# First layer's head of a four-stage hybrid kernel: one transfer for the projection, two folds in a row, the first batch in halves

## The chip, the cores and the metric

The kernel runs on one core of a Trainium2 chip, in float32 with some products in 16 bits. The metric is the device time of one execution in microseconds (us). In this text PE is TensorE, DVE is VectorE, ACT is ScalarE, POOL is GpSimd and SP is SyncE. Each runs its own list of instructions in order and waits on semaphores.

## What is computed

`x` is 2 batches of 512 rows with 256 channels. Four stages follow each other: attention, a feed-forward part, a state-space convolution, and the feed-forward part again, each with its own layer norm of what it reads. The change is in the first:

```python
x_norm = (x - mu) / jnp.sqrt(var + EPS) * gamma + beta
q = x_norm @ qkv[:, :KEY]
k = x_norm @ qkv[:, KEY:2 * KEY]
v = x_norm @ qkv[:, 2 * KEY:]
scores = jnp.einsum('bsk,btk->bst', q, k) * scale      # causal
attn = jax.nn.softmax(scores, axis=-1)
out = (attn @ v) @ o_proj + residual
```

The feed-forward part rounds its weights to an 8-bit grid first (`w.astype(jnp.float8_e4m3fn)`) and then computes `(silu(x @ gate * s) * (x @ up * s)) @ down * s`.

## The kernel before

The order of each engine's work is written out by hand; nothing reorders it. The 1,024 rows of `x` are eight tiles of 128 rows, numbered 0 to 7, four to a batch; the 256 channels are two chunks of 128.

**Head.** Instead of `q` and `k`, the kernel multiplies the weights once: `wqk` from `Wq` and `Wk`, `wvo` from `Wv` and `o_proj` (a "fold", L1047). Then the scores are `xn wqk xn^T` and the values `xn wvo`. For a fold PE turns the three thirds of `qkv` (`turn_w`, L1039) and ACT copies each from PSUM (`turned`, L492). Of `x`, DVE takes the statistics of two tiles at a time (`first_stats`, L707), POOL the inverse deviation (`inverse_std`, L285). Tiles 0 to 3 are normalised on DVE (`normalise`, L701), tiles 4 to 7 on ACT (L529). PE turns them (`turn_z`, L1054), and ACT (chunk 0) and DVE (chunk 1) apply gamma and beta on the way out of PSUM, giving `xn_cols` (`xn_chunk`, L497 and L712). `make_g` (L1062) gives `g = xn wqk` with 512 columns at a time, copied by `g_part` on ACT and `g_chunk` on DVE; `make_v` (L1071) gives the values, copied half by ACT (`v_part`), half by DVE (`v_half`, L723).

**Attention.** Per tile k: `scores(k)` on PE, `row_max(k)` on DVE (L853), the exponential on ACT (L562), `turn_probs(k)` on PE, `copy_probs(k)` on ACT, `attend(k)` on PE, `attention_out(k)` on DVE (L858). PE's order is `scores(k)`, `attend(k-2)`, `turn_probs(k-1)` (L1173); ACT's is `exp_scores(k)`, then `copy_probs(k-1)` (L592); DVE's is `row_max(k)`, then `attention_out(k-2)` (L897).

**Weights beside it.** While attention runs, the feed-forward weights are rounded. DVE makes a grid for each of the three weights, as two steps over 1,536 columns (`grid_begin`, `grid_end`, L773 to L781). For gate and up, POOL then adds and subtracts it in three pieces of 512 columns each (`round_weight`, L404); for down, DVE does that itself, with two operands in SBUF (`lift_down`, `lower_down`, L785 to L796). POOL also makes the scales of the residual (`x_plus_scales`, L393).

**Loads.** SP issues x, the thirds of `qkv`, the four parameter rows, `o_proj`, the scales and the weights on one queue (L238 to L251); ACT issues three small ones (L513 to L518), POOL two (L383). PE runs 14 transposes of the identity at the start and 8 more between the turning of q and of k (L1037, L1080).

## Time and profile before

| | us |
|---|---|
| median of 3 runs | 127.24 |
| lowest and highest | 127.01, 127.3 |
| the profiled execution | 127.35 |
| its span | 125.6 |
| PE busy in the span | 116.5 (93%) |
| DVE busy | 94.4 (75%) |
| POOL busy | 86.8 (69%) |
| ACT busy | 77.6 (62%) |

The head and the attention take the first 52 us of the span; the rest is the feed-forward parts and the convolution. The chain of waits follows the work that ended last back from the end, each step to what released it. A timeline row is a group of instructions in a row on an engine, with its start, its length and, in brackets, how long the engine stood idle before it and what ended that. The trace shows two records for each float32 product of PE (one for each transpose), the lists of the order one.

### The profile page before, as it was taken

The page shows a single profiled execution, that of the slowest core. Times are in us where ns is not written, and L with a number is a line of the kernel's source. Part 1 is how long each engine was busy: PE and PEld are TensorE (multiplying, and loading weights), DVE is VectorE, ACT ScalarE, POOL GpSimd, SP SyncE. Part 2 cuts the span into 40 slices and gives each one's busy share as a digit, 9 for nine tenths or more (in the row PEclk, how much of TensorE's full clock was granted, in tenths as well). Part 3 has the DMA queues.
Part 4 walks back from the last instruction along what each step waited for, and adds up shares of the span by engine and source line. Part 5 has one row for each costly group of instructions (what it writes and reads, how often), then busy time and mean ns, then how long its engine had stood idle before and what let it go on. Part 6 is the DMA issues. An engine that isn't in the chain of part 4 may idle for free.

```text
span 125.6 us, 2089 instructions
## 1 busy us (share of the span) xinstructions
PE 116.5 (93%) x666; PEld 77.3 (62%) x666; DVE 94.4 (75%) x226; ACT 77.6 (62%) x147; POOL 86.8 (69%) x168
## 2 busy tenths in 40 slices
PE   5997999999999999999999999989999869999970
PEld 5885468658668758745769545567446457556640
DVE  0398999919865866949797899947899946784592
ACT  2145079695875468858865278865578764579800
POOL 2246469999999888888433578889978870038831
PEclk9999999999999999999999999999999999999999
DMA  3998940000000000000000000000000000000404
GB/s 90 297 277 322 354 135 8 0 0 0 0 0 0 5 5 0 0 0 0 0 0 5 0 0 0 0 3 5 0 0 0 3 0 0 5 0 24 143 0 167
DMA packets 5682, 5.80 MB, mean 46 GB/s; under 512 B 1140, under 2 KB 5160, under 8 KB 5672
## 3 DMA queue, kind: packets, MB, share of 16 engines
q1 hardware_dynamic: 4648, 5.52, 13.3%
q10 hardware_dynamic: 960, 0.15, 0.7%
q8 instruction: 5, 0.08, 0.3%
q14 instruction: 5, 0.04, 0.1%
q0 software_dynamic: 64, 0.02, 0.1%
HBM read 4.63 MB, written 1.05 MB: 45 GB/s over the span
## 4 chain that ended last, share of the span: by engine, by line
PE 66%; DVE 11%; POOL 10%; ACT 4%; issue 3%; DMA 3%; SPq 0%; POOLq 0%; DVEq 0%; ACTq 0%
PE psum L1195 22%; PE psum L1211 10%; PE psum L1134 7%; PE psum L1109 7%; PE psum L1074 6%; POOL rstd L296 4%; DMA qkv_sb<-in_qkv 3%; PE psum L1067 3%; DVE stats L696 3%; PE psum L1156 2%; PE psum L1122 2%; POOL f_tail L451 2%; ACT h_rows L559 2%; ACT normed L529 2%; PE psum L1050 2%
## 5 line engine op out<-in xcount | busy, mean ns | idle before, releaser
L607 ACT ACTIVATE gated<-psum,scales 128x512 f32<-128x512 f32 x24 | 16.3, 681 | 13.1 <-PE psum L1195 13.1
L451 POOL TENSOR_TENSOR f_tail<-fused,f_head 128x512 f16<-128x512 f32 x12 | 14.1, 1173 | 12.8 <-ACT f_head L613 12.5
L1211 PE MATMUL psum<-down,f_head 128*128 128x256 bf16 x96 | 22.1, 273 | 0.5 <-POOL f_tail L451 0.5
L1211 PE MATMUL psum<-down,f_tail 128*128 128x256 bf16 x96 | 22.0, 272 | 0.0
L958 DVE SCALAR_TENSOR_TENSOR fused<-psum,up_scales_fit,gated 128x512 f32<-128x512 f32 (+1 forms) x25 | 17.8, 716 | 4.6 <-PE psum L1195 3.3
L613 ACT ACTIVATE f_head<-fused 128x512 f16<-128x512 f32 (+1 forms) x25 | 15.1, 606 | 3.4 <-DVE fused L958 3.2
L966 DVE TENSOR_TENSOR f_tail<-fused,f_head 128x512 f16<-128x512 f32 (+1 forms) x13 | 9.7, 749 | 9.2 <-ACT f_head L613 9.1
L1195 PE MATMUL psum<-h_head,up 128*128 128x512 f16 x48 | 14.3, 379 | 0.0
L1195 PE MATMUL psum<-h_tail,up 128*128 128x512 f16 x48 | 14.3, 379 | 0.0
L1195 PE MATMUL psum<-h_tail,gate 128*128 128x512 f16 x48 | 14.3, 379 | 0.0
L1195 PE MATMUL psum<-h_head,gate 128*128 128x512 f16 x48 | 14.3, 379 | 0.0
L296 POOL TENSOR_TENSOR rstd<-var_eps,neg_half 128x2 f32<-128x2 f32 (+1 forms) x15 | 12.3, 822 | 2.2
L1211 PEld LDWEIGHTS psum<-down,f_head 128*128 128x128 f16 x96 | 9.4, 98 | 4.2 <-POOL f_tail L451 1.8
L1134 PE MATMUL psum<-v_rows,probs_cols 128*128 128x256 f32 x40 | 10.3, 389 | 0.2 <-ACT probs_cols L575 0.2
L1211 PEld LDWEIGHTS psum<-down,f_tail 128*128 128x128 f16 x96 | 9.4, 98 | 1.6
L1109 PE MATMUL psum<-xn_cols,g_cols 128*128 128x128 f32 (+3 forms) x32 | 10.0, 436 | 0.0
L291 POOL TENSOR_SCALAR var_eps<-mean_var 128x2 f32<-128x2 f32 (+1 forms) x15 | 3.8, 255 | 8.8 <-DVE mean_var L699 7.7
L1134 PEld LDWEIGHTS psum<-v_rows,probs_cols 128*128 128x128 f32 x40 | 7.0, 190 | 2.3 <-ACT probs_cols L575 0.8
L1195 PEld LDWEIGHTS psum<-h_tail,gate 128*128 128x128 f16 x48 | 4.7, 98 | 5.7 <-DVE h_tail L850 0.2
L1195 PEld LDWEIGHTS psum<-h_tail,up 128*128 128x128 f16 x48 | 4.7, 98 | 5.7
L1195 PEld LDWEIGHTS psum<-h_head,up 128*128 128x128 f16 x48 | 4.7, 98 | 5.6
L1067 PE MATMUL psum<-xn_cols,wqk 128*128 128x512 f32 x16 | 7.4, 604 | 0.7 <-DVE xn_cols L715 0.7
(167 smaller groups left out, 257.2 us busy)
## 6 DMA issues: line engine op xcount, KB each, us to landing
x_in<-in_x SPq DMA_DIRECT2D x4, 256.0 KB, 4.2
qkv_sb<-in_qkv SPq DMA_DIRECT2D x3, 256.0 KB, 4.0
gate_raw<-in_gate_w SPq DMA_DIRECT2D x1, 768.0 KB, 6.8
up_raw<-in_up_w SPq DMA_DIRECT2D x1, 768.0 KB, 8.6
down_raw<-in_down_w SPq DMA_DIRECT2D x1, 768.0 KB, 10.3
out<-x_in SPq DMA_DIRECT2D x3, 256.0 KB, 2.1
wo_sb<-in_o_proj SPq DMA_DIRECT2D x1, 256.0 KB, 5.3
down_scale_all<-in_down_scale SPq DMA_DIRECT2D x1, 128.0 KB, 10.1
```

The costliest lines, as they stand in the source:

```text
L296: power = pool.tensor_tensor(rstd[:, n, k:k + count], var_eps[:, n, k:k + count], neg_half[:, 0:count], ALU.pow)
L451: pool.tensor_tensor(f_tail[:, m, :], fused[:, m % FUSED, :], f_head[:, m, :], ALU.subtract).then_inc(f_tail_by_pool, 1)
L607: act.activation(gated[:, m % 2, :], psum[:, BANK_GATE[m % 2], :], ACT.Silu, scale=gate_scales[:, m:m + 1]).then_inc(gated_ready, 1)
L613: act.activation(f_head[:, m, cols], fused[:, m % FUSED, cols], ACT.Copy).then_inc(f_head_ready, 1)
L958: dve.scalar_tensor_tensor(out=fused[:, m % FUSED, cols], in0=psum[:, BANK_UP[m % 2], cols], scalar=up_scales_fit[:, m:m + 1], in1=gated[: ...
L966: dve.tensor_tensor(f_tail[:, m, cols], fused[:, m % FUSED, cols], f_head[:, m, cols], ALU.subtract).then_inc(f_tail_by_dve, 1)
L1067: last = pe.matmul(column(BANK_G[b][j], 0, S), wqk[:, c, j * P:j * P + P], xn_cols[:, b, c, :], start=(c == 0), stop=(c == C - 1))
L1074: last = pe.matmul(column(BANK_V[b][t // 2], H * (t % 2), H), xn_cols[:, b, c, t * P:t * P + P], wvo[:, c, :], start=(c == 0), stop=(c == ...
L1109: pe.matmul(column(BANK_S[k % 2], 0, W), g_cols[:, b, j, i * P:i * P + P], xn_cols[:, b, j, 0:W], start=(j == 0), stop=(j == C - 1))
L1134: last = pe.matmul(column(BANK_O[k % 2], 0, H), probs_cols[:, k % 2, t * P:t * P + P], v_rows[:, b, t, :], start=(t == 0), stop=(t == i))
L1195: last = pe.matmul(column(banks[m % 2], 0, S), w[:, c, m * P:m * P + P], part[:, c, :], start=(part is h_head and c == 0), stop=(part is h ...
L1211: last = pe.matmul(down_columns(n, t), part[:, m, t * P:t * P + P], down16[:, m, :], start=(m == 0 and (t % 2 == 0 or n == 2 * B - 1) and ...
```

## The change

- SP loads the whole `qkv` in one transfer behind the first x, then x1, `o_proj`, x2, x3. Three parameter rows (gamma, beta, d) go to ACT's queue, ahead of its own loads; the fourth, `log_dt`, which nothing read, is gone. The two `c` loads go from POOL to the end of SP's queue.
- PE makes 17 warm-up transposes and none in between. It turns all three thirds in a row and makes both folds in a row. The copy of the turned k goes from ACT to DVE (`copy_k`).
- The first batch goes by halves of its tokens: `turn_z_half`, `xn_half` on ACT and DVE, `make_g_half` with 256 columns. The first half of `g` is copied by ACT alone, the second by DVE alone. `scores(0)` and `scores(1)` come ahead of the second half of `g`, of the values and of the second batch's `z`. `make_g_half(1)` writes the bank of the first values, so it waits for `v_by_act`.
- DVE copies the parameters, the turned k and the first half of `xn` ahead of `first_stats(2)`; `row_max(0)` and `row_max(1)` come ahead of the grids of up and down.
- POOL makes `x_plus_scales` ahead of `round_weight(0)`. ACT makes both first exponentials ahead of the last copy of `g` and the second square.

```diff
-WARM_UP = 14
-WARM_BETWEEN = 8
+WARM_UP = 17
...
-        BANK_G = [[6, 7], [0, 1]]
+        BANK_G = [[5, 2], [0, 1]]
...
             load_x(0)
-            load_chunks(qkv_sb[:, :, 0:KEY], qkv[:, 0:KEY], q_loaded)
+            load_chunks(qkv_sb[:], qkv, qkv_loaded)
             load_x(1)
-            load_chunks(qkv_sb[:, :, KEY:2 * KEY], qkv[:, KEY:2 * KEY], k_loaded)
-            load_rows(param_rows, (gamma, beta, log_dt, d_param), params_loaded)
-            load_chunks(qkv_sb[:, :, 2 * KEY:], qkv[:, 2 * KEY:], v_loaded)
+            load_chunks(wo_sb[:], o_proj, wo_loaded)
             load_x(2)
             load_x(3)
-            load_chunks(wo_sb[:], o_proj, wo_loaded)
             load_rows(scale_rows, (gate_scale, up_scale), scales_loaded)
             load_chunks(gate_raw[:], gate_w, w_loaded[0])
             load_chunks(up_raw[:], up_w, w_loaded[1])
             load_chunks(down_raw[:], down_w, w_loaded[2])
+            for n, array in ((2, c_re), (3, c_im)):
+                load_chunks(s4d_in[:, n, :].rearrange("p (c n) -> p c n", c=C), array, c_loaded)
             sp.dma_start(down_scale_all[:], down_scale.partition_broadcast(P)).then_inc(down_scale_loaded, 16)
...
-                load_s4d(2, c_re, c_loaded)
-                load_s4d(3, c_im, c_loaded)
...
             inverse_std(0, T, T, twice=True, negative_mean=True)
+            x_plus_scales()
             round_weight(0, gate16, gate_up_ready)
-            x_plus_scales()
             angle_squares()
...
+            def load_row(n, vector):
+                act.dma_start(param_rows[C * n:C * n + C, :],
+                              vector.rearrange("(m p) -> m p", p=P)).then_inc(params_loaded, 16)
...
+            load_row(0, gamma)
+            load_row(1, beta)
+            load_row(2, d_param)
...
             turned(0)
-            turned(1)
+            turned(2)
+            xn_half(0)
+            act.wait_ge(wqk_made, 1)
+            act.activation(wqk[:].rearrange("p c n -> p (c n)"), psum[:, BANK_WQK, :], ACT.Copy).then_inc(wqk_ready, 1)
+            act.wait_ge(wvo_made, 1)
+            act.activation(wvo[:].rearrange("p c n -> p (c n)"), psum[:, BANK_WVO, :], ACT.Copy).then_inc(wvo_ready, 1)
+            g_first_half()
...
+            xn_half(1)
...
-            act.wait_ge(wvo_made, 1)
-            act.activation(wvo[:].rearrange("p c n -> p (c n)"), psum[:, BANK_WVO, :], ACT.Copy).then_inc(wvo_ready, 1)
-            g_part(0)
-            xn_chunk(1)
+            v_part(0)
...
             act.activation(s4d[:, 12, 0:HN], s4d[:, 9, 0:HN], ACT.Sin, scale=0.5).then_inc(trig_out, 1)
-            v_part(0)
+            xn_second()
...
             exp_scores(0)
-            g_part(1)
+            exp_scores(1)
+            g_part()
             square_weights(1)
-            exp_scores(1)
...
+            def copy_k():
+                dve.wait_ge(w_turned_pe, 2)
+                dve.tensor_copy(w_turned[:, 1, :, :].rearrange("p c n -> p (c n)"),
+                                psum[:, BANK_WT[1], :]).then_inc(k_turned, 1)
+
+            def copy_params():
+                dve.wait_ge(params_turned, 1)
+                dve.tensor_copy(params[:], psum[:, BANK_PARAMS, 0:3 * C]).then_inc(params_ready, 1)
                 dve.wait_ge(params_ready, 1)
...
+            def xn_half(half):
+                dve.wait_ge(z_turned, half + 1)
+                dve.tensor_scalar(xn_cols[:, 0, 1, HALVES[half]], psum[:, BANK_Z[0][1], HALVES[half]], gammas[:, 1:2],
+                                  betas[:, 1:2], ALU.mult, ALU.add).then_inc(xn_by_dve, 1)
...
+            def g_second_half():
+                dve.wait_ge(g_made, 2)
+                dve.tensor_scalar(g_cols[:, 0, :, HALVES[1]], psum[:, BANK_G[0][1], :].rearrange("p (j s) -> p j s", j=C),
+                                  float(KEY) ** -0.5, None, ALU.mult).then_inc(g_by_dve, 1)
...
             first_stats(0)
             normalise((0, 1))
+            copy_params()
+            copy_k()
+            xn_half(0)
             first_stats(2)
+            first_stats(T)
+            normalise((2, 3))
+            first_stats(T + 2)
             exp_reduce()
-            normalise((2, 3))
-            dve.wait_ge(params_turned, 1)
-            dve.tensor_copy(params[:], psum[:, BANK_PARAMS, 0:4 * C]).then_inc(params_ready, 1)
+            xn_half(1)
             exp_finish()
-            xn_chunk(0)
-            first_stats(T)
-            first_stats(T + 2)
             exp_times_dt()
             reduce_angle()
             grid_begin(0)
             grid_end(0)
-            g_chunk(0)
+            row_max(0)
+            row_max(1)
+            g_second_half()
+            xn_second()
+            v_half(0)
             grid_begin(1)
-            xn_chunk(1)
             grid_end(1)
             grid_begin(2)
-            v_half(0)
-            row_max(0)
             grid_end(2)
-            row_max(1)
             lift_down(0)
-            g_chunk(1)
+            g_chunk()
             lift_down(1)
             lower_down(0)
             v_half(1)
...
+            def turn_w(w):
+                pe.wait_ge(qkv_loaded, 16)
...
+            def turn_z_half(half):
+
+                for t in (2 * half, 2 * half + 1):
+                    pe.wait_ge(z_ready, t + 1)
+                    for c in range(C):
+                        last = pe.transpose(column(BANK_Z[0][c], t * P, P),
+                                            normed[:, t, c * P:c * P + P], ident[:])
+                last.then_inc(z_turned, 1)
...
+            def make_g_half(half):
+
+                columns_there(half + 1)
                 for j in range(C):
                     for c in range(C):
-                        last = pe.matmul(column(BANK_G[b][j], 0, S), wqk[:, c, j * P:j * P + P], xn_cols[:, b, c, :],
+                        last = pe.matmul(column(BANK_G[0][half], j * (S // 2), S // 2), wqk[:, c, j * P:j * P + P],
+                                         xn_cols[:, 0, c, HALVES[half]], start=(c == 0), stop=(c == C - 1))
+                last.then_inc(g_made, 1)
...
-            turn_w(0, q_loaded)
-            warm_up(WARM_BETWEEN)
-            turn_w(1, k_loaded)
-
-            pe.wait_ge(params_loaded, 64)
-            pe.transpose(column(BANK_PARAMS, 0, 4 * C), param_rows[:], ident[0:4 * C, 0:4 * C]).then_inc(params_turned, 1)
-            turn_z(0, (0, 1))
-            pe.wait_ge(w_turned_ready, 2)
+            turn_w(0)
+            turn_w(1)
+            turn_w(2)
+
+            pe.wait_ge(params_loaded, 48)
+            pe.transpose(column(BANK_PARAMS, 0, 3 * C), param_rows[:], ident[0:3 * C, 0:3 * C]).then_inc(params_turned, 1)
+            turn_z_half(0)
+            pe.wait_ge(q_v_turned, 1)
+            pe.wait_ge(k_turned, 1)
             fold(BANK_WQK, 0, lambda kc: w_turned[:, 1, kc, :]).then_inc(wqk_made, 1)
-            turn_z(0, (2, 3))
-            turn_w(2, v_loaded)
-            pe.wait_ge(wqk_ready, 1)
-            pe.wait_ge(params_ready, 1)
-            make_g(0)
-            pe.wait_ge(w_turned_ready, 3)
+            pe.wait_ge(q_v_turned, 2)
             pe.wait_ge(wo_loaded, 16)
             fold(BANK_WVO, 2, lambda kc: wo_sb[:, kc, :]).then_inc(wvo_made, 1)
+            pe.wait_ge(wqk_ready, 1)
+            make_g_half(0)
+            turn_z_half(1)
+            pe.wait_ge(wvo_ready, 1)
+            make_v(0, (0, 1))
...
+                if k == 2:
                     pe.wait_ge(g_by_dve, 1)
...
                 if k == 0:
-                    pe.wait_ge(v_by_act, 1)
+                    pe.wait_ge(g_by_dve, 1)
                     pe.wait_ge(v_by_dve, 1)
...
-            turn_z(1)
-            pe.wait_ge(wvo_ready, 1)
-            make_v(0)
             scores(0)
-
+            scores(1)
+            pe.wait_ge(v_by_act, 1)
+            make_g_half(1)
+            turn_z()
+            make_v(0, (2, 3))
+
+            columns_there(3)
             pe.wait_ge(scales_loaded, 32)
-            pe.wait_ge(xn_by_act, 2)
             pe.transpose(column(BANK_SCALES, 0, 2 * M), scale_rows[:], ident[0:2 * M, 0:2 * M]).then_inc(scales_turned, 1)
-            make_g(1)
-            scores(1)
+            make_g()
             turn_probs(0)
             pe.wait_ge(scales_ready, 1)
             make_v(1)
```

DVE between its first `normalise` and the end of the second, before: L704 is `normalise`, L696 and L699 are statistics, L734 to L747 an exponential, L874 the copy of the parameters.

```order
L704 TENSOR_SCALAR normed<-x_in,mean_var,rstd 128x256 x2
L696 BN_STATS stats<-x_in 128x6 x2
L699 BN_AGGR mean_var<-stats 128x2 x2
L734 TENSOR_SCALAR s4d<-e_in 128x18
L735 TENSOR_SCALAR s4d<-s4d 128x18
L736 SCALAR_TENSOR_TENSOR s4d<-s4d,e_in 128x18
L737 SCALAR_TENSOR_TENSOR s4d<-s4d 128x18
L738 TENSOR_SCALAR s4d<-s4d 128x18
L739 TENSOR_SCALAR two_k<-s4d 128x18
L704 TENSOR_SCALAR normed<-x_in,mean_var,rstd 128x256 x2
L874 COPY params<-psum 128x8
```

And now, where L713 is `normalise`, L728 the parameters, L723 `copy_k`, L733 `xn_half`, L705 and L708 statistics.

```order
L713 TENSOR_SCALAR normed<-x_in,mean_var,rstd 128x256 x2
L728 COPY params<-psum 128x6
L723 COPY w_turned<-psum 128x512
L733 TENSOR_SCALAR xn_cols<-psum,params 128x256
L705 BN_STATS stats<-x_in 128x6 x2
L708 BN_AGGR mean_var<-stats 128x2 x2
L705 BN_STATS stats<-x_in 128x6 x2
L708 BN_AGGR mean_var<-stats 128x2 x2
L713 TENSOR_SCALAR normed<-x_in,mean_var,rstd 128x256 x2
```

The copies of the parameters and of k, which wait for PE, now stand ahead of the statistics of all tiles but the first two; the exponential stands behind them.

DVE from the first `g` copy to the second, before: L776 and L781 are the grids, L715 `xn_chunk`, L725 `v_half`, L855 `row_max`, L789 `lift_down`.

```order
L720 TENSOR_SCALAR g_cols<-psum 128x512
L776 TENSOR_SCALAR grid<-up_raw 128x1536
L715 TENSOR_SCALAR xn_cols<-psum,params 128x512
L781 TENSOR_SCALAR grid<-grid 128x1536
L776 TENSOR_SCALAR grid<-down_raw 128x1536
L725 COPY v_rows<-psum 128x512
L855 TENSOR_REDUCE neg_max<-psum 128x1
L781 TENSOR_SCALAR grid<-grid 128x1536
L855 TENSOR_REDUCE neg_max<-psum 128x1
L789 TENSOR_TENSOR down_raw<-down_raw,grid 128x768
L720 TENSOR_SCALAR g_cols<-psum 128x512
```

And now, from `row_max(0)` on: L883 is `row_max`, L743 and L748 copies of `g`, L738 `xn_second`, L753 `v_half`, L804 and L809 the grids, L817 `lift_down`.

```order
L883 TENSOR_REDUCE neg_max<-psum 128x1 x2
L743 TENSOR_SCALAR g_cols<-psum 128x2x256
L738 TENSOR_SCALAR xn_cols<-psum,params 128x512
L753 COPY v_rows<-psum 128x512
L804 TENSOR_SCALAR grid<-up_raw 128x1536
L809 TENSOR_SCALAR grid<-grid 128x1536
L804 TENSOR_SCALAR grid<-down_raw 128x1536
L809 TENSOR_SCALAR grid<-grid 128x1536
L817 TENSOR_TENSOR down_raw<-down_raw,grid 128x768
L748 TENSOR_SCALAR g_cols<-psum 128x512
L817 TENSOR_TENSOR down_raw<-down_raw,grid 128x768
```

The four grid steps of up and down, which had copies and row maxima between them, now stand in a row behind `v_half(0)`.

PE from the first `g` to the second batch's, before: L1067 is `make_g`, L1050 a fold, L1058 `turn_z`, L1074 `make_v`, L1109 and L1111 scores, L1167 the turned scales.

```order
L1067 MATMUL psum<-xn_cols,wqk 128x512 x4
L1050 MATMUL psum<-wo_sb,w_turned 128x256 x4
L1058 MATMUL psum<-ident,normed 128x128 x8
L1074 MATMUL psum<-wvo,xn_cols 128x256 x8
L1109 MATMUL psum<-xn_cols,g_cols 128x128 x2
L1111 MATMUL psum<-mask,ident 128x128
L1167 MATMUL psum<-ident,scale_rows 128x12
L1067 MATMUL psum<-xn_cols,wqk 128x512 x4
```

And now: L1109 is `make_g_half`, L1096 and L1087 turn `z`, L1123 is `make_v`, L1161 and L1163 scores, L1221 the scales, L1116 `make_g`.

```order
L1109 MATMUL psum<-xn_cols,wqk 128x256 x4
L1096 MATMUL psum<-ident,normed 128x128 x4
L1123 MATMUL psum<-wvo,xn_cols 128x256 x4
L1161 MATMUL psum<-xn_cols,g_cols 128x128 x2
L1163 MATMUL psum<-mask,ident 128x128
L1161 MATMUL psum<-xn_cols,g_cols 128x256 x2
L1163 MATMUL psum<-mask,ident 128x128
L1109 MATMUL psum<-xn_cols,wqk 128x256 x4
L1087 MATMUL psum<-ident,normed 128x128 x8
L1123 MATMUL psum<-wvo,xn_cols 128x256 x4
L1221 MATMUL psum<-ident,scale_rows 128x12
L1116 MATMUL psum<-xn_cols,wqk 128x512 x4
```

Two tiles of scores now stand ahead of the second halves of `g` and `v` and of the second batch's `z`.

## Rows read from the trace of the kernel before

**Rows 1.** Chain of waits (start us, us, what), 7 to 39 us.

```profile
7.37 0.44 PE psum L1043 x4
...
13.48 0.26 DVE mean_var L699 x2
...
16.49 2.09 ACT normed L529 x4
...
23.48 3.63 PE psum L1067 x8
...
28.15 3.46 PE psum L1074 x16
31.60 1.29 PE psum L1109 x4
...
37.41 1.56 PE psum L1134 x6
```

**Rows 2.** Window 37.40 to 52.45: its length, PE busy (instructions), clock, DMA.

```profile
37.40:52.45 15.05, 15.04 (x96) 1.00 0.01 2
```

**Rows 3.** Landing of `qkv`; issue of k on SP's queue; the page's GB/s.

```profile
DMA to landing us min/median/max: 3.7/4.0/4.3
...
2.23 0.47 SPq L229 DMA_DIRECT2D qkv_sb<-in_qkv  x1
...
GB/s 90 297 277 322 354 135 8 0 0 0 0 0 0 5 5 0 0 0 0 0 0 5 0 0 0 0 3 5 0 0 0 3 0 0 5 0 24 143 0 167
```

**Rows 4.** Timeline of PE, the first 6 us.

```profile
1.52 3.25 PE L1035 MATMUL psum<-ident 128*128 128x128 f32 x14 [1.52 <-POOL ident L277]
4.98 1.12 PE L1043 MATMUL psum<-ident,qkv_sb 128*128 128x128 f32 x4 [0.21 <-DMA qkv_sb<-in_qkv]
```

**Rows 5.** Timeline of DVE, two groups of its head.

```profile
6.68 0.74 DVE L696 BATCH_NORM_STATS2 stats<-x_in 128x6 f32<-128x256 f32 x2
...
15.44 0.95 DVE L776 TENSOR_SCALAR grid<-gate_raw 128x1536 uint32<-128x1536 uint32 x1
```

**Rows 6.** Timelines of DVE and POOL, weight steps, 17 to 42 us.

```profile
17.91 1.65 DVE L776 TENSOR_SCALAR grid<-up_raw 128x1536 uint32<-128x1536 uint32 x1
...
20.65 1.99 POOL L408 TENSOR_TENSOR x<-gate_raw,grid 128x512 f32<-128x512 f32 x1
...
21.43 2.03 DVE L776 TENSOR_SCALAR grid<-down_raw 128x1536 uint32<-128x1536 uint32 x1
...
32.86 3.73 POOL L408 TENSOR_TENSOR scaled_down<-up_raw,grid 128x512 f32<-128x512 f32 x3
...
40.14 1.08 DVE L795 TENSOR_TENSOR down_raw<-down_raw,grid 128x768 f32<-128x768 f32 x1
...
40.49 0.78 POOL L291 TENSOR_SCALAR var_eps<-mean_var 128x2 f32<-128x2 f32 x1
41.35 0.19 POOL L293 TENSOR_SCALAR mean_rstd<-mean_var 128x2 f32<-128x2 f32 x1
```

**Rows 7.** Timeline of POOL, first long and last step of `x_plus_scales`.

```profile
28.13 1.66 POOL L396 TENSOR_TENSOR rstd<-var_eps,neg_half 128x8 f32<-128x8 f32 x1
...
31.13 0.79 POOL L399 TENSOR_SCALAR neg_x_plus<-mean_rstd 128x8 f32<-128x8 f32 x1
```

**Rows 8.** Timeline of DVE, 23 to 36 us.

```profile
23.38 0.68 DVE L725 COPY v_rows<-psum 128x512 f32<-128x512 f32 x1
...
28.07 0.42 DVE L855 TENSOR_REDUCE neg_max<-psum 128x1 f32<-128x256 f32 x1 [2.67 <-PE psum L1111]
...
32.98 0.56 DVE L855 TENSOR_REDUCE neg_max<-psum 128x1 f32<-128x384 f32 x1 [0.53 <-PE psum L1111]
...
34.63 0.18 DVE L699 BATCH_NORM_AGGREGATE mean_var<-stats 128x2 f32<-128x6 f32 x1
...
35.47 0.69 DVE L855 TENSOR_REDUCE neg_max<-psum 128x1 f32<-128x512 f32 x1 [0.66 <-PE psum L1111]
```

77 lines of the change are left out of this document (40 added, 37 removed).

## The prediction, made before the changed kernel was run

> **What bounds the kernel now.** Start with the chain of waits. From 19 us on it is TensorE (PE) alone: the two big products of the second batch, 3.63 and 3.46 us, and the scores of tile 2 at 31.60 follow each other without a gap [rows 1]. Ahead of that it is a relay: the first third of `qkv`, 3.7 us after its issue [rows 3], transposes, a fold, then at 13.48 VectorE's (DVE's) statistics, POOL, and ScalarE's (ACT's) four `normed` rows until 18.58 [rows 1]. The next view is PE by windows: from 37.40 to 52.45, where the feed-forward part begins, PE is busy 15.04 of 15.05 us [rows 2]. So whatever the head loses or gains by the time `attend(2)` starts (37.41 [rows 1]) is handed on whole. The last view is DVE's timeline: it waits 2.67 us for the scores of tile 1 [rows 8], so today DVE's weight work (`grid`, `lift`, `lower`) is paid out of idle time. That is the number to keep an eye on, because the change moves this work.
>
> **The transfer and the start.** The three thirds of `qkv` landed 3.7, 4.0 and 4.3 us after issue, the first being 3.7, and the second was issued at 2.23, so it was there at 6.2 to 6.5 [rows 3]. By then the queue had moved x0, q, x1 and k, 1,024 KB, the same bytes as x0 and the whole `qkv`. I take 6.35 for the new landing. Worked out another way, `qkv` is 786,000 bytes behind x0 (there at 3.7): at the 354 GB/s of the page's fifth slice that is 2.2 us, 5.9; at the 277 of the third 2.8 us, 6.5, and 0.3 more if the first bytes come late, 6.8 [rows 3]. PE's 17 warm-up transposes at 3.25/14 = 0.23 us are over by 5.5, so PE waits about 0.9 us. Twelve transposes at 0.44 per four [rows 1] are 1.3 us, with 0.2 for the first two, as the clock was still at its lower level until about 6.7: four transposes at 4.98 took 1.12 us [rows 4]. They end at 7.9, the parameters' transpose and `z` half 0 at 8.5. Loads that move to ACT's queue: three issues put its table load 1.5 us later, to about 5 us, and its first copy is wanted at 7.2, so that costs nothing; the two `c` loads leave POOL and land behind `down_raw`, long before `taps_begin`: nothing.
>
> **PE to its first stop.** The fold now needs `copy_k` from DVE, and DVE stands at `copy_params` from 6.7 (it began `first_stats(2)` at 6.68 before [rows 5]) until the parameters are turned at 8.2. 0.15 and 0.6 us (a 512-column PSUM copy is 0.68 [rows 8]) later, at 9.1, the fold starts. From there in a row: the fold's 8 matmuls of 256 columns, 1.73 by the 3.46 us for 16 [rows 1] and 0.15 to start, 1.9; second fold 1.73, `make_g_half(0)` 1.73, `z` half 1 0.44, `make_v` on two tiles 1.73, scores 0 and 1 1.4: 18.0. Then PE waits for `v_by_act`. DVE, 9.05: `xn_half` 0.4, two `first_stats` 1.9, `normalise` 0.9, the last statistics 1.0, 13.2. From there to ACT's first `normed` took 13.74 to 16.49 = 2.75 us and the four took 2.09 [rows 1]; with `v_part` 0.6 this is 18.7. PE: wait 0.7, `g` half 1 1.73, `turn_z` 0.87, `make_v` 1.73: second half of `v` at 23.2. Then 0.16, 3.5 and 3.6 us: `scores(2)` starts at about 30.3, against 31.60 [rows 1]. **By PE alone the change gains 1.3 us.**
>
> **DVE, where I think it is lost.** `grid_begin(0)` started at 15.44 [rows 5]. Now DVE has stood 1.5 us at `copy_params` and made an extra 0.6 us copy, so it starts at 18.1 and ends the pair at 20.0; `round_weight(0)` on POOL starts at 20.1 (`x_plus_scales`, now ahead of it, took from about 28 to 31.9 [rows 7] and would run 16.0 to 20.1). Two row maxima, `g_second_half` and `xn_second` follow, then DVE waits for `v` until 23.2 and is free at 23.9. Only now come `grid` 1 and 2, the two lifts, `g_chunk`, the lower and `v_half(1)`, and behind them `row_max(2)`.
>
> How long is that? Alone, a `grid` piece is 0.95 us [rows 5] and a POOL piece 3.73/3 = 1.24 [rows 6]. Side by side they were 1.65 and 2.03 on DVE and 1.99 on POOL [rows 6]. The ends tell why: the POOL piece of 20.65 ended at 22.64, the DVE piece that had been asked for at 21.43 ended 0.82 later, at 23.46. They do not slow each other, they take turns, and a DVE piece that finds POOL at the start of a piece costs that piece without its start-up, 1.24 less 0.1, and its own 0.82: 1.95 us. Before, PSUM copies lay between the DVE pieces and hid POOL's turns; now four stand in a row. The two-input steps take turns too: `lower_down(1)` at 40.14 took 1.08 and POOL's small step at 40.49 took 0.78 until DVE was done [rows 6], when the like step at 41.35 took 0.19.
>
> The sum from 23.9: POOL's first three pieces are just over (20.1 + 3.7), so `grid_begin(1)` 0.95; three more at 1.95 each, against POOL's other three, 5.85; `lift_down(0)` 0.9 beside POOL's small angle steps (as long as a `grid` piece alone, less the overlap with the next), `g_chunk` 0.6, `lift_down(1)` 0.9; by 32.3 POOL has begun on `up`, so `lower_down(0)` takes a turn behind it, 1.95; `v_half(1)` 0.6. `row_max(2)` starts at 35.65 against 32.98 [rows 8], although its scores are there at 31.7. Next: `row_max(3)` stands behind `attention_out(0)`, 1.8 us (32.98 to the end of the statistics at 34.81 [rows 8]), so 37.45. From its start to `attend(2)` took 35.47 to 37.41, 1.94 us [rows 1, 8], through ACT's exponential and copy. `attend(2)` starts at 39.4 against 37.41: **+1.9 to 2.0 us**. I take 1.9, as the halves of `xn` may be a shade shorter than I allowed. PE's waits behind it were 0.01 us [rows 2], so nothing is given back. The profiled execution (127.35) would become 129.25, the median of the runs, 0.11 lower, 129.1.
>
> The Trainium skill (SBUF — State Buffer, Who interferes with whom) says the same of the pair: VectorE in a two-port mode, or with two SBUF inputs against a GpSimd step that reads SBUF, and GpSimd hold a shared port pair one at a time, and the second "fully blocks". By that rule, the trace agrees: 2.03 us for a 0.95 us step. The rule speaks against putting DVE's `grid` pieces back to back beside POOL's. It also names the two-input steps: without a turn for `lower_down(0)` the sum would be 1 us lower, 128.1.
>
> **Rivals.** (1) *Faster: the turns do not bite.* If POOL and DVE run past each other (POOL late or early by its six pieces), DVE's block from 23.9 is 4 x 0.95 + 2.9 + 1.2 = 7.9 us, over at 31.8, as the scores of tile 2 land. Then PE's gain of 1.3 stands: 125.9. It decides at the point where the block is under 8 us. For it: the row of [rows 5] at 0.95. Against it: POOL's six pieces are six times 1.24 = 7.5 us from 20.1, so they must overlap it. (2) *Half the price:* the two-input steps escape POOL's second round because it starts later than 33: 1.1 us less, 128.0. (3) *The clock rises later.* PE was busy almost without a break from 1.52 until it rose [rows 4]; now it stands idle from 5.5 to 6.4. If it stays at the lower level for the transposes and the first fold (0.23 to 0.28 against 0.11 a transpose), 1.2 us are added: 130.3. (4) *Nothing:* DVE's block of about 9.7 us eats exactly PE's gain, 127.2. That one transfer lands later than two thirds did is in the range (0.25 us of the sum for 0.45 of landing, since part is under `v_by_act`).
>
> **Chances.** Forecast, with its ends at 128.3 and 129.9: 50%. Rival 3: 14%. Rival 2: 12%. Rival 1: 16%. Rival 4 or close to it: 8%. A measurement here can tell about 0.2% (0.25 us). So slower by more than that 76%, the same 8%, faster 16%. The range leaves out rival 1 and the worst of rival 3: 127.4 to 130.6.
>
> **What would show it.** Right: in the profile of the changed kernel `grid` pieces of L804 and L809 take about 2 us in three of the last four, `row_max(2)` starts near 35.6, PE has a wait of some 3 us ahead of `attend(1)` whose releaser is ACT's `probs_cols`, behind DVE's `neg_max`, and `scores(2)` starts near 30.3 all the same. The `qkv` landing is at 5.9 to 6.8 and the fold starts near 9.1. Wrong: `row_max(2)` waiting for its scores instead of being late for them (rival 1), or twelve transposes that take over 2 us (rival 3).

## The result, and the profile of the changed kernel

The change makes the kernel slower, and by far more than forecast.

| kernel | median us | lowest to highest | ratio to before |
|---|---|---|---|
| before | 127.16 | 127.01 to 127.30 | |
| changed | 133.18 | 131.31 to 134.18 | 1.037 (1.031 to 1.043) |

The ratio is taken over undisturbed executions alone, so it is lower than the quotient of the medians. The profiled execution took 132.64 us with a span of 130.8, against 127.35 and 125.6: 5.3 us more.

The first thing to look at is the page's line of PE's granted clock, in 40 slices of the span, for before and then for the changed kernel. A 9 stands for 90% of full speed or more.

```profile
PEclk9999999999999999999999999999999999999999
PEclk9999999999965799999999999999999999999997
```

The timeline of PE in the changed kernel (start us, us, engine, line, operation, tiles, count, and in brackets the idle time ahead with its releaser) shows where that is:

```profile
29.73 1.45 PE L1161 MATMUL psum<-xn_cols,g_cols 128*128 128x384 f32 x4
...
33.51 0.22 PE L1163 MATMUL psum<-mask,ident 128*128 128x128 bf16 x1
37.99 2.07 PE L1186 MATMUL psum<-v_rows,probs_cols 128*128 128x256 f32 x4 [4.27 <-ACT probs_cols L584]
39.86 0.85 PE L1174 MATMUL psum<-ident,probs 128*128 128x128 f32 x3
...
41.46 2.81 PE L1186 MATMUL psum<-v_rows,probs_cols 128*128 128x256 f32 x6
...
57.58 0.59 PE L1248 MATMUL psum<-h_head,gate 128*128 128x512 f16 x2
```

The same places in before:

```profile
31.44 1.45 PE L1109 MATMUL psum<-xn_cols,g_cols 128*128 128x384 f32 x4
...
35.27 1.08 PE L1134 MATMUL psum<-v_rows,probs_cols 128*128 128x256 f32 x4
...
37.41 1.56 PE L1134 MATMUL psum<-v_rows,probs_cols 128*128 128x256 f32 x6 [0.23 <-ACT probs_cols L575]
...
52.28 0.59 PE L1195 MATMUL psum<-h_head,gate 128*128 128x512 f16 x2
```

And PE by windows in the changed kernel (start and end, length, PE busy with its instructions, granted clock, DMA share, GB/s):

```profile
29.73:33.72 3.99, 3.99 (x15) 1.00 0.00 0
33.72:37.99 4.27, 0.01 (x1) 0.91 0.00 0
37.99:44.11 6.12, 6.12 (x19) 0.50 0.00 0
44.11:57.75 13.64, 13.64 (x91) 1.00 0.01 2
```

`scores(2)` does start earlier, at 29.73 against 31.44. But then PE stands for 4.27 us ahead of attend(1), and when it may go on, the clock is granted at 0.50, the lower of its two levels (1.2 GHz instead of 2.4), for 6.12 us. The same matmuls (attend(1), three transposes, `scores(4)`, attend(2)) took 3.30 us at the full clock in before, 35.27 to 38.80 less a wait of 0.23. So the sum up to the feed-forward part, which starts at 57.58 against 52.28, is: -1.71 for the earlier scores, +4.27 for the wait, +2.82 for the clock, -0.23 for the wait that before had there. That is 5.15 of 5.30 us. (The other 0.16 is in the row of windows ahead of the wait: 3.99 us from `scores(2)` on, where before had 3.83 from 31.44 to 35.27.)

DVE's timeline shows what PE waited for:

```profile
7.80 0.17 DVE L728 COPY params<-psum 128x6 f32<-128x6 f32 x1 [1.09 <-PE psum L1133]
8.00 0.69 DVE L723 COPY w_turned<-psum 128x512 f32<-128x512 f32 x1
...
17.94 0.94 DVE L804 TENSOR_SCALAR grid<-gate_raw 128x1536 uint32<-128x1536 uint32 x1
...
22.58 0.69 DVE L753 COPY v_rows<-psum 128x512 f32<-128x512 f32 x1 [0.86 <-PE psum L1123]
23.19 1.32 DVE L804 TENSOR_SCALAR grid<-up_raw 128x1536 uint32<-128x1536 uint32 x1
24.54 1.91 DVE L809 TENSOR_SCALAR grid<-grid 128x1536 f32<-128x1536 f32 x1
26.37 2.02 DVE L804 TENSOR_SCALAR grid<-down_raw 128x1536 uint32<-128x1536 uint32 x1
28.43 1.92 DVE L809 TENSOR_SCALAR grid<-grid 128x1536 f32<-128x1536 f32 x1
30.38 1.02 DVE L817 TENSOR_TENSOR down_raw<-down_raw,grid 128x768 f32<-128x768 f32 x1
...
31.93 2.04 DVE L817 TENSOR_TENSOR down_raw<-down_raw,grid 128x768 f32<-128x768 f32 x1
33.99 1.90 DVE L823 TENSOR_TENSOR down_raw<-down_raw,grid 128x768 f32<-128x768 f32 x1
...
36.42 0.54 DVE L883 TENSOR_REDUCE neg_max<-psum 128x1 f32<-128x384 f32 x1
...
38.14 0.66 DVE L883 TENSOR_REDUCE neg_max<-psum 128x1 f32<-128x512 f32 x1
```

Five of the seven weight steps last about 1.95 us, where [rows 5] had 0.95 for one alone, and `row_max(2)` comes at 36.42 against 32.98 [rows 8]. POOL's timeline beside it has its `gate` pieces from 19.96 to 29.5 and `up` from 31.88, 0.05 us ahead of DVE's second lift:

```profile
19.96 3.73 POOL L400 TENSOR_TENSOR x<-gate_raw,grid 128x512 f32<-128x512 f32 x3 [1.95 <-DVE grid L809]
23.77 5.76 POOL L403 TENSOR_TENSOR gate<-x,grid 128x512 f16<-128x512 f32 x3
...
31.88 5.13 POOL L400 TENSOR_TENSOR scaled_down<-up_raw,grid 128x512 f32<-128x512 f32 x3
```

### The profile page after: what moved, and what is told of

It reads as the page before. It is cut to its first block, busy times and chain, and to the rows that moved or that the text cites. A ratio compares the mean times of both kernels' runs of the same rounds, so it can differ in the third digit from the quotient of the medians.

```text
span 130.8 us, 2095 instructions
## 1 busy us (share of the span) xinstructions
PE 118.0 (90%) x669; PEld 80.1 (61%) x669; DVE 98.1 (75%) x228; ACT 77.7 (59%) x147; POOL 84.8 (65%) x166
## 3 DMA queue, kind: packets, MB, share of 16 engines
HBM read 4.63 MB, written 1.05 MB: 43 GB/s over the span
## 4 chain that ended last, share of the span: by engine, by line
PE 58%; DVE 19%; POOL 8%; ACT 5%; issue 5%; DMA 3%; SPq 0%; POOLq 0%; DVEq 0%
PE psum L1248 21%; PE psum L1264 10%; PE psum L1186 8%; PE psum L1161 4%; DMA qkv_sb<-in_qkv 3%; POOL rstd L290 3%; DVE grid L809 3%; PE psum L1109 3%; PE psum L1079 3%; DVE grid L804 2%; PE psum L1208 2%; DVE down_raw L817 2%; PE psum L1174 2%; POOL f_tail L443 2%; ACT h_rows L568 2%
## 5 line engine op out<-in xcount | busy, mean ns | idle before, releaser
L1186 PE MATMUL psum<-v_rows,probs_cols 128*128 128x256 f32 x40 | 12.6, 454 | 4.3 <-ACT probs_cols L584 4.3
L290 POOL TENSOR_TENSOR rstd<-var_eps,neg_half 128x2 f32<-128x2 f32 (+1 forms) x15 | 12.8, 856 | 2.2
L1186 PEld LDWEIGHTS psum<-v_rows,probs_cols 128*128 128x128 f32 x40 | 8.3, 226 | 6.8 <-ACT probs_cols L584 4.8
L1161 PE MATMUL psum<-xn_cols,g_cols 128*128 128x128 f32 (+3 forms) x32 | 10.4, 456 | 0.0
L285 POOL TENSOR_SCALAR var_eps<-mean_var 128x2 f32<-128x2 f32 (+1 forms) x15 | 3.2, 216 | 10.5 <-DVE mean_var L708 9.5
L576 ACT ACTIVATE probs<-psum,neg_max 128x128 f32<-128x128 f32 (+3 forms) x8 | 4.2, 526 | 9.7 <-DVE neg_max L883 9.7
```

The costliest lines, as they stand in the source:

```text
L290: power = pool.tensor_tensor(rstd[:, n, k:k + count], var_eps[:, n, k:k + count], neg_half[:, 0:count], ALU.pow)
L576: act.activation(probs[:, k % 2, 0:W], psum[:, BANK_S[k % 2], 0:W], ACT.Exp, bias=neg_max[:, k:k + 1], accum_out=row_sum[:, k:k + 1]).then ...
L1161: pe.matmul(column(BANK_S[k % 2], 0, W), g_cols[:, b, j, i * P:i * P + P], xn_cols[:, b, j, 0:W], start=(j == 0), stop=(j == C - 1))
L1186: last = pe.matmul(column(BANK_O[k % 2], 0, H), probs_cols[:, k % 2, t * P:t * P + P], v_rows[:, b, t, :], start=(t == 0), stop=(t == i))
```

## Experiments on the clock

Theory: the wait costs its own length and then the clock. Rival: the wait alone, with the rest of the loss somewhere else. One kernel leaves every engine but PE as it is in the changed kernel; two make a wait in the kernel before.

**a1_fill**, the changed kernel with work for PE in the wait:

```diff
                 scores(k)
+                if k == 3:
+                    pe.wait_ge(g_by_dve, 2)
+                    for _ in range(34):
+                        pe.transpose(column(BANK_O[1], 0, P), ident[:], ident[:])
                 attend(k - 2)
```

> The changed kernel with 34 transposes of the identity on PE between the scores of tile 3 and attend(1), into the bank that attend(1) will overwrite, so that PE's 4.27 us wait is filled and nothing else moves. Theory (the wait makes PE's clock fall to its lower level for 6.8 us, and that is some 3 us of the loss): attend(1) starts at 38.0 as in the changed kernel, PE's products behind it take the short times, the feed-forward part starts near 55.1 instead of 57.75, and the time is 129.8. Rival (the lateness of DVE alone costs all of it, the clock nothing): 133 as the changed kernel.

Measured: 130.44 us median (128.71 to 131.51), ratio 1.018 (1.012 to 1.023). PE's timeline:

```profile
33.60 3.88 PE L1231 MATMUL psum<-ident 128*128 128x128 f32 x34
38.07 1.13 PE L1186 MATMUL psum<-v_rows,probs_cols 128*128 128x256 f32 x4 [0.59 <-ACT probs_cols L584]
```

attend(1) starts at 38.07, as late as in the changed kernel, but takes 1.13 us instead of 2.07, and the clock of the profiled execution is 1.0 throughout. The feed-forward part starts 2.6 us earlier (55.00) without one useful instruction more. Between the two profiled executions the time falls by as much, from 132.64 to 130.07 us. The clock's share of the loss is 2.6 us, and the theory holds.

**b1_long** and **b2_short**, the kernel before with spare steps on DVE, 17 and 11 of them:

```diff
             v_half(1)
+            for n in range(17):
+                dve.bn_stats(spare[:, n, :], x_in[:, n % K, :])
             for k in range(2, K):
```

> The kernel before with 17 spare statistics steps (5.6 us) on DVE ahead of row_max(2), so that PE waits over 4 us ahead of attend(1), as in the changed kernel; nothing of the change is in it. Clock theory: DVE's lateness costs 4.4 us and the fallen clock about 3 more, 134.5. Rival (no clock): 131.6.

> The same with 11 spare steps (3.6 us): PE waits about 2.3 us ahead of attend(1). Clock theory, if the shorter wait leaves the clock up: 127.2 + 2.4 = 129.6; if the clock falls here too, 132 or more. Rival without a clock: 129.6 as well, so this run only says from which length of the wait the price is paid.

Measured: 132.78 us (132.76 to 133.87), ratio 1.047 (1.043 to 1.050), with 17; 130.00 us (129.30 to 131.03), ratio 1.023 (1.018 to 1.029), with 11. `attend(1)` behind the wait, b1_long's and then b2_short's:

```profile
39.41 1.89 PE L1137 MATMUL psum<-v_rows,probs_cols 128*128 128x256 f32 x4 [4.08 <-ACT probs_cols L576]
```

```profile
37.37 1.13 PE L1137 MATMUL psum<-v_rows,probs_cols 128*128 128x256 f32 x4 [2.12 <-ACT probs_cols L576]
```

A wait of 4.08 us on PE brings the lower clock in a kernel that has nothing of the change in it; here the price was 1.4 us: 132.78 less b2_short's 129.37 (both profiled executions), less the 1.96 us by which the wait is longer. I had expected about 3 us and 134.5, so half of the price did not come: the granted clock was low for 3.18 us here and for 6.12 us in the changed kernel. The low stretch is not of one length, and why is open. After 2.12 us the profiled execution kept its clock. But 2 us are no safe side: of b2_short's other three executions two had a mean clock of 0.987 and 0.980 and took 131.03 and 130.62 us, the third 1.0 and 129.30. (These have no trace, so where in them the clock was low is not shown.)

## Experiments on DVE's block

**a2_order**, the changed kernel with lifts and lowers behind the first attention tiles:

```diff
-            lift_down(0)
             g_chunk()
-            lift_down(1)
-            lower_down(0)
             v_half(1)
...
                 if k == 4:
-                    lower_down(1)
+                    lift_down(0)
+                    lift_down(1)
                     magnitude()
+                if k == 5:
+                    lower_down(0)
+                if k == 6:
+                    lower_down(1)
```

> The changed kernel with DVE's two lifts and the first lower of the down weight moved from ahead of row_max(2) to behind attention_out(2), (3) and (4), where DVE waits anyway. Theory (the changed kernel's loss is DVE's block ahead of row_max(2), in turns with POOL, and the clock that follows from PE's wait): row_max(2) starts at 31.6 with its scores just there, PE waits under 1 us, the clock stays, the feed-forward part starts at 50.6 to 51.0 and the time is 125.4 to 125.8, under the kernel before. Rival (the halves and the single transfer cost by themselves): 127.2 or more.

Measured: 127.07 us (126.55 to 127.46), ratio 0.999 (0.996 to 1.002). Between the profiled executions (132.64 and 126.81) 5.8 us are won back by moving DVE's steps on the `down` weight. In its trace `row_max(2)` stands at 31.33, when its scores are there, and the feed-forward part at 51.75 against 52.28 of before. The four `grid` steps still take turns (1.32 to 2.03 us) but end by 30.2: not the turns by themselves, but the turns with three more steps behind them made `row_max(2)` late. DVE's row, and then three smaller waits of PE:

```profile
31.33 0.54 DVE L883 TENSOR_REDUCE neg_max<-psum 128x1 f32<-128x384 f32 x1
```

```profile
35.57 1.56 PE L1188 MATMUL psum<-v_rows,probs_cols 128*128 128x256 f32 x6 [0.23 <-ACT probs_cols L584]
...
45.25 1.13 PE L1188 MATMUL psum<-v_rows,probs_cols 128*128 128x256 f32 x4 [0.35 <-ACT probs_cols L584]
...
47.79 0.66 PE L1176 MATMUL psum<-ident,probs 128*128 128x128 f32 x4 [0.65 <-ACT probs L576]
```

The first was there before; the other two, 1.0 us, are the lowers, now ahead of the row maxima of tiles 6 and 7. With them the feed-forward part starts 0.75 to 1.15 us later than the expected 50.6 to 51.0, and the expected 125.4 to 125.8 did not come.

**a3_pool_later**: are the turns with POOL the reason that the block is long, or the seven steps as such?

```diff
-            round_weight(0, gate16, gate_up_ready)
             angle_squares()
-            round_weight(1, up16, gate_up_ready)
+            pool.wait_ge(v_by_dve, 2)
+            round_weight(0, gate16, gate_up_ready)
             inverse_std(1, 0, 2, negative_mean=True)
+            round_weight(1, up16, gate_up_ready)
```

> The changed kernel with POOL's rounding of `gate` and `up` begun only when DVE has done `v_half(1)`, so that none of POOL's 128x512 pieces lies beside DVE's block; DVE's order and PE's are untouched. Theory (the turns with POOL made the block long, the wait of 4.27 us it led to took the clock): the four `grid` pieces from 23 us and the three `down` pieces take 0.95 us each, `row_max(2)` waits for its scores at about 31.1 instead of being late at 36.4, PE waits under 1 us ahead of attend(1), the granted clock stays at 1.0 and the time is 125.3 to 126.0. If the block is long for another reason (its place behind `v_half(0)`, its own seven pieces), `row_max(2)` stays behind 34 and the time above 130. POOL's later rounding can cost up to 1 us near 46 us, where `h_rows` needs its small steps.

Measured: 135.59 us (134.29 to 136.20), ratio 1.063 (1.057 to 1.069). The time missed and the mechanism hit. DVE's block and `row_max(2)`:

```profile
22.74 0.95 DVE L805 TENSOR_SCALAR grid<-up_raw 128x1536 uint32<-128x1536 uint32 x1
23.73 0.96 DVE L810 TENSOR_SCALAR grid<-grid 128x1536 f32<-128x1536 f32 x1
...
30.84 0.56 DVE L884 TENSOR_REDUCE neg_max<-psum 128x1 f32<-128x384 f32 x1 [0.23 <-PE psum L1164]
```

With POOL silent every one of the seven steps takes 0.95 us, and the row maximum waits for its scores, as in before. PE ran ahead and met a new wait at the far end:

```profile
55.08 1.12 PE L1209 MATMUL psum<-ident,h_rows 128*128 128x128 f32 x4 [6.94 <-ACT h_rows L569]
```

POOL's later `up` rounding ends at 48.0, and behind it in POOL's queue stand the taps, the weight bound and then the inverse deviations of tiles 2 and 3 that `h_rows` needs, at 52.2. I had put up to 1 us on that place; it was 6.94 us, and the clock fell again behind it (the four transposes took 1.12 us instead of 0.60).

**c1_row**, the kernel before with one part of the change alone, the `grid` steps in a row:

```diff
-            grid_begin(1)
             xn_chunk(1)
-            grid_end(1)
-            grid_begin(2)
             v_half(0)
             row_max(0)
+            grid_begin(1)
+            grid_end(1)
+            grid_begin(2)
             grid_end(2)
             row_max(1)
```

> The kernel before with one part of the change alone: DVE's pieces of `grid` 1 and 2 stand in a row behind `v_half(0)` and `row_max(0)`, ahead of `row_max(1)`. Theory: they start at 24.4; POOL's first six pieces run until 28, so two of the four take 1.3 and 1.95 us and the others 0.95; `row_max(1)` starts at 29.8 (28.07 before), `row_max(2)` 1.7 us late at 34.7, PE waits under 2.1 us and keeps its clock: 128.7 to 129.2. Rival (the order costs nothing, as DVE idles 2.67 us there anyway): 127.2.

Measured: 127.15 us (127.02 to 127.80), ratio 0.999 (0.996 to 1.002). My theory missed by 1.6 to 2 us. DVE and POOL:

```profile
23.37 0.95 DVE L776 TENSOR_SCALAR grid<-up_raw 128x1536 uint32<-128x1536 uint32 x1
24.36 1.91 DVE L781 TENSOR_SCALAR grid<-grid 128x1536 f32<-128x1536 f32 x1
26.19 0.95 DVE L776 TENSOR_SCALAR grid<-down_raw 128x1536 uint32<-128x1536 uint32 x1
```

```profile
20.98 4.47 POOL L411 TENSOR_TENSOR gate<-x,grid 128x512 f16<-128x512 f32 x3
25.54 0.79 POOL L395 TENSOR_SCALAR var_eps<-mean_var 128x8 f32<-128x8 f32 x1
```

One step of four took a turn: with no DVE step between them POOL's pieces ended at 25.45, not 28, and what POOL did next was small. DVE stood there idle anyway. So a row of steps is not the fault by itself. With a3_pool_later it says that the fault is the row at the time of POOL's pieces. In the changed kernel these began at 19.96 instead of 17.47, since `grid_begin(0)` began at 17.94 instead of 15.44 [rows 5].

**a4_x_plus_behind** undoes one part of the change, on POOL:

```diff
-            x_plus_scales()
             round_weight(0, gate16, gate_up_ready)
+            x_plus_scales()
```

> The changed kernel with one part undone: POOL's `x_plus_scales` stands behind its rounding of `gate` again, as before the change. In the changed kernel POOL's six `gate` pieces begin at 19.96 us either way (they wait for `grid`), but its `up` pieces would now begin some 2.5 us later, behind 34 us. Theory: the four `grid` pieces keep their turns, the last two two-input steps (2.04 and 1.90 us in the changed kernel) fall to about 1.0 each, `row_max(2)` moves from 36.4 to 34.5, PE's wait from 4.27 to 2.3 us, and because the wait is shorter the granted clock does not fall: 127.6 to 128.6. Rival (the clock falls after any wait of that kind): 131 and more. Rival (`x_plus` comes too late for attention_out(0) and holds it): wait as long as before, 133.

Measured: 131.00 us (129.12 to 131.44), ratio 1.023 (1.016 to 1.030). DVE did what was expected to 0.1 us, ACT and PE did not. The rows are DVE's, ACT's and PE's:

```profile
32.02 0.95 DVE L817 TENSOR_TENSOR down_raw<-down_raw,grid 128x768 f32<-128x768 f32 x1
33.00 0.96 DVE L823 TENSOR_TENSOR down_raw<-down_raw,grid 128x768 f32<-128x768 f32 x1
...
34.48 0.55 DVE L883 TENSOR_REDUCE neg_max<-psum 128x1 f32<-128x384 f32 x1
```

```profile
34.51 2.08 ACT L561 ACTIVATE x_plus<-x_in,neg_x_plus,one_rstd 128x256 f32<-128x256 f32 x4 [5.32 <-POOL neg_x_plus L391]
```

```profile
37.47 1.95 PE L1186 MATMUL psum<-v_rows,probs_cols 128*128 128x256 f32 x4 [3.58 <-ACT probs_cols L584]
```

The two-input steps lose their turns and `row_max(2)` comes at 34.48. But ACT's four `x_plus` rows now stand ahead of its exponential and start when POOL lets them, so that PE still waits 3.58 us, and the clock falls (1.95 us for 1.08). In the execution of 129.12 us, which has no trace, the mean clock was 1.0. So POOL's new order costs two turns and spares PE this wait for ACT; undoing it gains 1.8 us between the profiled executions (132.64 and 130.85), not the whole 5.3.

## Attempts at a version that beats both

Four kernels build on the changed head. **w1_spread** puts single DVE steps into DVE's waits. **w2_block_free** computes the `grid` of `gate` at 13 us and that of `up` behind the `down` steps, so that POOL rounds ahead of the block and behind it. **w3_taps_behind** adds POOL's inverse deviations ahead of its taps. **w4_warm** adds two warm-up transposes. w2_block_free and the two built on it also have `first_stats(2)` ahead of `copy_params`, as w1_spread has. The core of w2_block_free:

```diff
             exp_reduce()
+            grid_begin(0)
+            grid_end(0)
             xn_half(1)
...
             v_half(0)
-            grid_begin(1)
-            grid_end(1)
             grid_begin(2)
             grid_end(2)
             lift_down(0)
             g_chunk()
             lift_down(1)
             lower_down(0)
+            grid_begin(1)
+            grid_end(1)
             v_half(1)
```

And what w3_taps_behind does on POOL:

```diff
-            taps_begin()
...
             inverse_std(1, 2, 2, negative_mean=True)
+            taps_begin()
```

> The changed kernel with DVE's weight work spread: `first_stats(2)` ahead of `copy_params` (into the wait of 1.09 us), `grid_begin(1)` ahead of `v_half(0)` (into the wait of 0.86 us), `g_chunk` between the `grid` pieces, the lifts and lowers of `down` one by one among the attention tiles (k = 4, 4, 5, 7). Theory: `row_max(2)` waits for its scores (31.1), PE's waits up to 52 us add up to under 1 us, clock 1.0: 125.4 to 126.2. Rival: POOL's turns on the spread pieces hold the row maxima of tiles 5 to 7 back as they did with three pieces (0.2 to 0.7 us each): 126.6 to 127.3.

> The changed kernel with DVE's order changed so that POOL's twelve pieces and DVE's block stand one after the other: `first_stats(2)` ahead of `copy_params`, `grid` of `gate` at about 12.6 us (into DVE's wait for `z`), so that POOL rounds `gate` from 16.4 to 24; behind `v_half(0)` the `down` weight's grid, lifts and lower first and `grid` of `up` last, so that POOL's `up` pieces begin after the block. Theory: the seven pieces of the block take 0.95 us but for the first (a turn at 23 us), `row_max(2)` waits for its scores (31.1), PE has no wait over 1 us, clock 1.0, the feed-forward part begins at 50.5 to 51.5 and the time is 125.3 to 126.3. Rival (another chain takes the gain, as in the run with POOL's rounding later): a wait on `h_rows` near 47 us of over 1 us, 126.5 to 127.5.

> As the kernel with the free block, and on POOL the small steps of the taps (about 3 us) moved behind the inverse deviations of tiles 2 and 3, which ACT's second pair of `h_rows` waits for. Theory: what is left of the wait on `h_rows` near 47 us goes; 125.2 to 125.8, at or below the kernel with the free block. Rival: the taps were hidden there: the same time as that kernel within 0.3 us.

> As the kernel with the taps behind, and 19 warm-up transposes on PE instead of 17 (2 x 0.23 us), which fills the gap of 0.3 to 0.6 us until `qkv` lands. Theory: executions in which PE stands idle there get their full clock later, and these make the spread of the changed kernels (up to 1 us); with the gap filled the spread falls to that of the kernel before (0.3 us) at the same lowest time. Rival: the spread has another cause and stays.

The table has two more kernels, which are told of below it.

| kernel | median us | lowest to highest | ratio to before |
|---|---|---|---|
| w1_spread | 127.40 | 127.19 to 128.11 | 1.002 (1.000 to 1.004) |
| w2_block_free | 127.28 | 126.07 to 128.35 | 1.001 (0.998 to 1.004) |
| w3_taps_behind | 127.29 | 126.20 to 130.02 | 0.999 (0.996 to 1.003) |
| w4_warm | 127.07 | 125.77 to 128.52 | 0.999 (0.996 to 1.002) |
| w5_trig_first | 126.78 | 126.21 to 127.83 | 0.998 (0.996 to 1.000) |
| w6_thirds | 128.43 | 128.15 to 130.24 | 1.017 (1.011 to 1.023) |

The first four miss their expectation, though in their traces DVE's block holds PE up for a quarter of a microsecond at most ahead of `attend(1)` and `attend(2)`; the best executions of the last three of them, 125.77 to 126.20, are near it.

w1_spread's time is its rival's (127.40 for 126.6 to 127.3), but not by the rival's way. PE's waits that the rival named are small (0.26 and 0.60 us), and the feed-forward part starts at 51.57, 0.7 us earlier than in before. That gain is lost 10 us later: `lower_down(1)`, now at 48.35, holds POOL's rounding of `down` back (49.45 for 48.63 in before), some of POOL's small steps behind it take longer too, and POOL ends the taps of the convolution so late (61.43 for 60.15) that PE waits for them:

```profile
61.48 1.16 PE L1278 MATMUL psum<-ident,taps 128*128 128x128 f32 x8 [0.25 <-POOL taps L373]
```

The products behind these start 11.03 us after the feed-forward part's first, where before had 10.40. w2_block_free's median lies in its rival's range, but in its trace, a faster execution (126.54), the rival's wait on `h_rows` is not there. In w3_taps_behind the rival came in (the taps were hidden), and w4_warm's spread of 2.75 us says that two more transposes do not cure it. Two causes can be read in the traces of the last three. First, in w2_block_free DVE's small angle steps now lie beside POOL's pieces and take turns with them too, so that ACT's `xn` of the second batch comes late (DVE, then PE):

```profile
17.40 1.65 DVE L792 SCALAR_TENSOR_TENSOR s4d<-s4d 128x16 f32<-128x16 f32 x3
19.09 1.19 DVE L793 TENSOR_SCALAR s4d<-s4d 128x16 f32<-128x16 f32 x1
```

```profile
22.86 0.23 PE L1221 MATMUL psum<-ident,scale_rows 12*128 12x12 f32 x1 [0.55 <-ACT xn_cols L501]
```

These four steps took 0.80 us in the changed kernel, and 2.84 here. Second, `qkv` lands at different times. PE's first use of it in w3_taps_behind:

```profile
7.21 1.67 PE L1072 MATMUL psum<-ident,qkv_sb 128*128 128x128 f32 x12 [1.91 <-DMA qkv_sb<-in_qkv]
```

It was 5.69 in the changed kernel, 5.64 to 5.86 in seven others, 6.98 in w4_warm. In w3_taps_behind the granted clock then fell as well (mean 0.59 from 9.1 to 12.5 us), and this execution took 130.02 us. In before, PE needs a third at 5 us and has other work until it needs the next. Two more runs took one cause each: **w5_trig_first** lets POOL begin its `gate` pieces only behind the angle steps, **w6_thirds** loads the three thirds in a row on top of that.

```diff
             x_plus_scales()
+            pool.wait_ge(trig_in, 1)
             round_weight(0, gate16, gate_up_ready)
```

```diff
-            load_chunks(qkv_sb[:], qkv, qkv_loaded)
+            for w in range(3):
+                load_chunks(qkv_sb[:, :, w * KEY:w * KEY + KEY], qkv[:, w * KEY:w * KEY + KEY], third_loaded[w])
```

> As the kernel with the taps behind and 19 warm-up transposes, and POOL begins its rounding of `gate` only when DVE's small angle steps are done (they took a turn each: the last ended at 20.2 us instead of 17.9). Theory: ACT's `xn` of the second batch comes 1 us earlier, PE's wait of 0.55 to 2.0 us ahead of the second batch's product goes, 0.5 us less than the kernel it is made from: 126.5. Executions whose `qkv` lands late stay late by that much. Rival: POOL, begun later, takes turns with more of DVE's block and gives it back: 127.1.

> As that kernel, but `qkv` is loaded in three transfers in a row, each third with its own semaphore, as the only part of the changed head that is undone. Theory (the single transfer's last byte varies between executions, 5.65 to 7.2 us, and all twelve transposes wait for it): with thirds PE can do eight transposes ahead of the last third, the median falls by up to 0.3 us and the highest time by more: 126.2. Rival: the last third lands as late as the whole, and what waits for it (the fold's `k` and `v`) is the same: equal to the single transfer within 0.2 us.

w5_trig_first has the lowest median, 0.3 us below its base and between its theory and its rival, but its interval still touches 1: not told from the kernel before. Its trace is of its slowest execution (127.83). The wait for ACT's `xn` is gone there, but three of DVE's steps in the block take a turn (1.28, 1.91 and 1.91 us) and PE waits 1.05 us ahead of `attend(1)`, which is the rival; it also waits 1.29 us for ACT's `v_rows`, after DVE had waited 1.77 us for late rows of x. w6_thirds is 1.6 us slower, and not for the reason under test. In its trace the second x is issued 1.0 us later than in w5_trig_first (2.74 for 1.71), since the issues of three thirds take SP's queue 1.48 us where one transfer takes 0.46. It lands at 8.17, and DVE's statistics, which stand ahead of the copy of `k` in these kernels, waited 1.65 us for it, so the fold waited 1.48 us. (The same rows can be late with a single transfer too: w3_taps_behind's trace has a wait of 1.61 us for them.) The twelve transposes had no wait but took 2.31 us, where w5_trig_first's took 1.53. Whether thirds would cure the late landings stays open, as does the cause of the landings' spread. No version here beats the kernel before by more than can be measured.

## Why the prediction was wrong, step by step

**Landing and start: right, a little pessimistic.** Forecast 6.35 (5.9 to 6.8), measured 5.65; the wait was 0.3 us, not 0.9; the twelve transposes ended at 7.5 (7.9), the fold began at 8.84 (9.1) behind DVE's copy of `k`, as said. The transposes took 1.92 us for my 1.5, near the sign of rival 3 (over 2 us), but the first fold took 1.97 as before (1.99), so that rival's 1.2 us did not come. (The profile gives the granted clock as 1.00 from the start on, also where a warm-up transpose takes 0.23 us; that the lower level lasted until 6.7 us in before is my reading of durations, and no clock row shows it.) Over all traces of the changed head the landing is 5.6 to 7.2, wider than my range.

**PE alone: right in kind, short in size.** Scores 0 and 1 ended at 17.9 (18.0). The wait of 0.7 us for `v_by_act` was not there (0.05 us), because ACT's `normed` began at 15.34 instead of 15.95. So `scores(2)` started at 29.73, not 30.3: a gain of 1.7 us where I had 1.3. One sum of mine is off here: 18.7 and 1.73, 0.87 and 1.73 are 23.0, not 23.2; the 30.3 goes by the right one, DVE's 23.9 by the wrong one.

**DVE's block: right in kind, one turn short.** `grid_begin(0)` at 17.94 (18.1), `v_half(0)` over at 23.2 (23.9). Three `grid` steps took 1.91 to 2.02 (1.95 each). The first took 1.32 for my 0.95, since POOL was not "just over" but in its second half; `lift_down(1)` took 2.04 for my 0.9, since POOL's `up` pieces began at 31.88, 0.4 us before I had put them, and 0.05 before the lift. Together 1.5 us, against 0.7 for the earlier start: `row_max(2)` at 36.42 instead of 35.65. The rule of the Trainium skill (SBUF — State Buffer, Who interferes with whom) was borne out for the two-input steps (2.04 and 1.90 us beside POOL's pieces, 0.95 and 0.96 in a3_pool_later without them), and rivals 1 and 2 were wrong. POOL's `x_plus_scales` took 2.7 us (15.33 to 18.01) where I had 4.1; `round_weight(0)` began at 19.96 (20.1) all the same, since it waited for the `grid`.

**The step that failed: the way from PE's wait to the feed-forward part, priced at a full clock.** In the prediction's words: "From its start to `attend(2)` took 35.47 to 37.41, 1.94 us", and then "PE's waits behind it were 0.01 us [rows 2], so nothing is given back". I had named the wait ("some 3 us ahead of `attend(1)`") and added up only its length; the lower clock behind it was a term that I put at nothing without a reason. Both rows were measured behind a PE that had not stood still. Behind a wait of 4.27 us the matmuls up to attend(2)'s end took 6.12 us for 3.30, and this came in at two places:

- `row_max(3)` began at 38.14 for my 37.45: 0.7 us, which is DVE's block. From there to `attend(2)` it was 3.32 us, not 1.94: not ACT's chain set its start, but PE's own slow products ahead of it. That is 1.4 us.
- From `attend(2)` to the feed-forward part it was 16.12 us (41.46 to 57.58), where before had 14.87 (37.41 to 52.28): 1.25 us, the slow clock in `attend(2)` itself (2.81 us for 1.56).

The profiled execution was forecast at 129.25; with 0.7, 1.4 and 1.25 the sum is 132.6, and 132.64 was measured. a1_fill, where the clock stays up, is the same sum without the last two: 129.95, and its profiled execution took 130.07. My only rival on the clock was one at the start, where PE did not wait long.

**The sign** was right, and by the mechanism given first: a2_order takes the two lifts and a lower from in front of `row_max(2)` and the loss is gone.
